# Moving the bias add and the lower ELU branch of an eight-head attention layer from VectorE to GpSimd

## The reference

```python
x = _layernorm(x + L0(x))   # relational GCN, three layers
x = _layernorm(x + L1(x))   # GCN, two layers
x = _layernorm(x + L2(x))   # graph attention, 4 heads of 256, then 1 head of 768
x = _layernorm(x + L3(x))   # graph attention, 8 heads of 96, then 1 head of 768
```

```python
h = (x @ W).reshape(n, heads, out_c)
e = leaky_relu(al_s[src] + al_d[dst], 0.2)
ex = jnp.exp(e - segment_max(e, dst)[dst])
alpha = ex / (segment_sum(ex, dst)[dst] + 1e-16)
out = segment_sum(h[src] * alpha[:, :, None], dst) + bias
h = jax.nn.elu(out)          # out where out > 0, exp(out) - 1 elsewhere
```

## Time and profile before

| | |
|---|---|
| median of three runs | 1627.55 us (1625.88 to 1627.65) |
| the profiled execution | 1625.69 us |
| its span | 1624.0 us |
| mean granted TensorE clock | 0.95 |
| busy: TensorE | 1468.5 us, 90% |
| busy: VectorE | 803.1 us, 49% |
| busy: ScalarE | 427.7 us, 26% |
| busy: GpSimd | 501.6 us, 31% |

### The profile page before, as it was taken

The page is one execution under the profiler, slowest core; times in us unless marked ns, Lnnn a source line. Parts: engine busy times, 40 slices in busy tenths (PEclk is TensorE's granted clock), DMA queues, the critical chain, the costliest instruction groups (busy, mean ns, idle before and its releaser), DMA issues.

```text
span 1624.0 us, 23395 instructions
## 1 busy us (share of the span) xinstructions
PE 1468.5 (90%) x8072; PEld 1347.3 (83%) x8072; DVE 803.1 (49%) x1940; ACT 427.7 (26%) x1009; POOL 501.6 (31%) x574
## 2 busy tenths in 40 slices
PE   5899799999999999999999998988699788778896
PEld 3567699999999999999998897976589748677773
DVE  7888644224534465732234444175522053588544
ACT  1153511101000001001012214345523442544422
POOL 5111322332424443344234221471116441200020
PEclk9998899999999999999999998999899899777998
DMA  3110111212342232422122112221012200100001
GB/s 115 38 30 14 36 39 30 59 41 77 103 131 84 83 113 78 137 68 59 30 59 68 40 32 67 81 69 33 1 52 59 64 10 24 44 1 1 10 1 47
DMA packets 57526, 86.53 MB, mean 53 GB/s; under 512 B 6437, under 2 KB 54053, under 8 KB 57303
## 3 DMA queue, kind: packets, MB, share of 16 engines
q1 hardware_dynamic: 45184, 66.02, 14.0%
q10 hardware_dynamic: 12244, 19.17, 3.9%
HBM read 83.24 MB, written 1.92 MB: 52 GB/s over the span
## 4 chain that ended last, share of the span: by engine, by line
PE 74%; DVE 15%; ACT 5%; issue 3%; DMA 1%; POOL 1%; DVEq 0%; ACTq 0%; SPq 0%
PE psum L2005 12%; PE psum L2008 11%; PE psum L2009 11%; PE psum L2022 7%; PE psum L2025 7%; PE psum L2418 7%; PE psum L2343 3%; PE psum L2347 3%; PE psum L2348 3%; PE psum L2110 2%; ACT psum L1059 2%; PE psum L2407 1%; DVE onehot_dst L1314 1%; DVE max_scratch L1759 1%; PE psum L2066 1%
## 5 line engine op out<-in xcount | busy, mean ns | idle before, releaser
L2005 PE MATMUL psum<-w_lo,xT_hi 128*125 128x384 f32 (+1 forms) x1110 | 382.0, 344 | 6.8 <-ACT packed_sums L867 3.2
L2008 PE MATMUL psum<-w_hi,xT_lo 128*125 128x384 f32 (+1 forms) x1110 | 377.8, 340 | 0.0
L2009 PE MATMUL psum<-w_hi,xT_hi 128*125 128x384 f32 (+1 forms) x1110 | 377.2, 340 | 0.0
L741 POOL CAST w_hi<-w_raw 128x384 fp32r<-128x384 f32 x190 | 102.8, 541 | 502.6 <-PE psum L2009 492.5
L754 POOL TENSOR_TENSOR w_lo<-w_raw,w_hi 128x384 fp32r<-128x384 f32 x106 | 108.2, 1050 | 432.7 <-ACT w_hi L1037 321.4
L1350 DVE TENSOR_TENSOR h_lo<-psum,h_hi 125x384 fp32r<-125x384 f32 (+1 forms) x120 | 66.9, 558 | 316.3 <-ACT h_hi L895 315.3
L2005 PEld LDWEIGHTS psum<-w_lo,xT_hi 128*125 128x125 f32 (+1 forms) x1110 | 209.2, 188 | 9.3 <-ACT packed_sums L867 3.7
L2008 PEld LDWEIGHTS psum<-w_hi,xT_lo 128*125 128x125 f32 (+1 forms) x1110 | 209.1, 188 | 0.1
L2009 PEld LDWEIGHTS psum<-w_hi,xT_hi 128*125 128x125 f32 (+1 forms) x1110 | 208.6, 188 | 0.0
L2022 PE MATMUL psum<-h_lo,adjacency 125*125 125x384 f32 (+3 forms) x600 | 204.3, 340 | 1.8 <-ACT adjacency L935 1.7
L743 POOL TENSOR_TENSOR w_lo<-w_raw,w_hi 128x384 fp32r<-128x384 f32 x190 | 200.7, 1056 | 15.2
(11 more groups left out here) (284 smaller groups left out, 2244.7 us busy)
## 6 DMA issues: line engine op xcount, KB each, us to landing
w_raw<-weights_dram SPq DMA_DIRECT2D x296, 192.0 KB, 2.4
score_w_raw<-weights_dram ACTq DMA_DIRECT2D x58, 192.0 KB, 2.9
x_nat<-x_dram SPq DMA_DIRECT2D x1, 1875.0 KB
x_residual<-x_dram SPq DMA_DIRECT2D x1, 1875.0 KB
out_dram<-x_residual SPq DMA_DIRECT2D x5, 375.0 KB
score_a_rows<-L_gnn_a_src_dram ACTq DMA_DIRECT2D x8, 192.0 KB, 3.4
score_a_rows<-L_gnn_a_dst_dram ACTq DMA_DIRECT2D x8, 192.0 KB, 4.7
rgcn_bias<-rgcn_bias_dram SPq DMA_DIRECT2D x1, 1125.0 KB
```

The costliest lines, as they stand in the source:

```text
L741: nc.gpsimd.tensor_copy(mem.wh[:, slot, :], mem.raw[:, raw_slot, :]).then_inc(w_hi_ready, 1)
L2005: ins = nc.tensor.matmul(o, h, wl, start=(j == 0), stop=False, skip_group_check=True)
L2008: nc.tensor.matmul(o, l, wh, start=False, stop=False, skip_group_check=True)
L2009: ins = nc.tensor.matmul(o, h, wh, start=False, stop=stop and j == k - 1, skip_group_check=True)
```

## The change

For each head GpSimd now adds the bias, after VectorE's multiplication (part_read), and tells ScalarE (elu_in). When the exponential is there (elu_out) GpSimd makes its lower branch, min(e, 1) - 1, and tells VectorE through a new semaphore, elu_low. VectorE only joins the branches. The splits of the weight chunks, which GpSimd did in one go ahead of this, are put between the heads: index 15 ahead of head 0, 16 to 19 ahead of head 1, 20 ahead of head 2, the last three after head 7.

```diff
@@ gpsimd
             split_to(Q2.chunk + 15)
-            split_to(Q2.end + AHEAD)
+            pool.wait_ge(params_loaded, 16 * 9)
+            for h in range(HEADS3):
+                split_to(min(Q2.chunk + 16 + 4 * h, Q2.end + AHEAD))
+                e, t = mem.elu[0:BP, h % 2, :, :], strip(h)
+                b = mem.par[1][0:BP, h * C3:(h + 1) * C3].rearrange("p (a c) -> p a c", a=1).to_broadcast([BP, NB, C3])
+                pool.wait_ge(part_read, Q2.unit0 + h + 1)
+                nc.gpsimd.tensor_tensor(t, t, b, ALU.add).then_inc(elu_in, 1)
+                pool.wait_ge(elu_out, h + 1)
+                nc.gpsimd.tensor_scalar(e, e, 1.0, -1.0, ALU.min, ALU.add).then_inc(elu_low, 1)
             split_to(NCHUNKS)
@@ vector
                 nc.vector.tensor_tensor(t, head_out(h)[:, :, 0:C3], mem.z[0:BP, :, h % 2:h % 2 + 1].to_broadcast([BP, NB, C3]),
                                         ALU.mult).then_inc(part_read, 1)
-                dve.wait_ge(part_read, Q2.unit0 + h + 1)
-                b = mem.par[1][0:BP, h * C3:(h + 1) * C3].rearrange("p (a c) -> p a c", a=1).to_broadcast([BP, NB, C3])
-                nc.vector.tensor_tensor(t, t, b, ALU.add).then_inc(elu_in, 1)
 
             def head_elu(h):
 
-                dve.wait_ge(elu_out, h + 1)
+                dve.wait_ge(elu_low, h + 1)
                 e, t = mem.elu[0:BP, h % 2, :, :], strip(h)
-                link(nc.vector.tensor_scalar(e, e, 1.0, -1.0, ALU.min, ALU.add))
                 nc.vector.scalar_tensor_tensor(t, t, 0.0, e, ALU.max, ALU.add).then_inc(layer_ready, 1)
```

More of the change, by code:

```diff
@@ L544, in program @@
         elu_out = sem("elu_out")
+        elu_low = sem("elu_low")
         T_Q = [T_L1 + (1 + i) * UNITS for i in range(4)]
```

## The result

The changed kernel takes 1643.53 us, the median of four runs (1642.37 to 1643.74), against 1627.60 us of the kernel before on the same chip: a ratio of 1.0099, with a 95% interval of 1.0086 to 1.0111. It is 16 us slower. The prediction had 1629.6 us and a range up to 1635.0 us, so the time lies 8.5 us above the range. The profiled execution took 1643.74 us with a span of 1642.0 us, 18.0 us above the span before. One execution of add_alone, a kernel of this study, took 5510.57 us and is left out of its ratio.

The account below looks back on a forecast made before the run. No engine alone was the bound, but a loop of handoffs with VectorE's part largest. Loop -1.1, splits +2.3 and tail +0.9 summed to +2.1 us, from a median of 1627.55 to 1629.6 us; range 1621.0 to 1635.0 us.

Parts of the forecast that it names:

- The low branch: GpSimd's min(e, 1) - 1 in each head: 0.68 us, scaled from a cast, with bounds of 0.41 and 1.22 us.
- J: Start of VectorE's joining instruction in each head; its moves were to sum to -1.1 us over the loop.
- E: End of ScalarE's exponential in each head; the join could not start before E + 0.78 us.
- its step: Forecast move of the join's start in heads 0 to 5: -0.28, -0.39, +0.11, +0.11, -0.27, -0.39 us.
- rival A: Slower: GpSimd's low branch costs 1.22 us, deciding from about 0.85 us on; 1633.8 us in all, chance 0.20.
- The splits: Five weight splits moved behind low branches block the joins of heads 0 and 1 and a L1829: +2.3 us, bounds 0 and 4.
- the sum: Loop -1.1, moved splits +2.3 and tail +0.9 us: +2.1 us in all, median 1629.6 us.
- rival C: TensorE's clock: three more groups of sums at the low level give 1632.9 us (chance 0.13), three fewer 1626.3 us (0.10).
- the tail: Serial stretch behind the last head up to TensorE's next-layer transposes: add +0.56, low branch +0.27, handoffs +0.07, together +0.9 us.
- B: Faster: VectorE's own work is the bound, 7.9 us go and the tail's 0.9 comes; 1620.6 us, chance 0.15.
- The add: GpSimd's bias add in each head: 1.22 us, with its blocking of VectorE put at nothing.
- The joins of heads 0 and 1: VectorE's joins, each waiting 0.9 us for a moved split, were to last about 1.5 us.

Follow-up runs that it names:

- add_alone: Changed kernel with VectorE making the low branch again, so GpSimd only adds the bias, and the splits made first: 1626.84 us, ratio 0.9998.
- splits_alone: Kernel before with only the weight splits moved between the heads, VectorE doing all its old work: 1638.29 us, ratio 1.0070.
- low_fast_first: Changed kernel with multiply and add for minimum and add in GpSimd's low branch, and the splits made first: 1627.96 us, ratio 1.0007.
- low_fast: Changed kernel with multiply and add for minimum and add in GpSimd's low branch, splits still between the heads: 1634.69 us, ratio 1.0056.
- the two fused kernels: Kernel before without a separate low branch, the join giving ELU plus 1: bias add on VectorE 1624.9 us, on GpSimd 1621.85 us.
- splits_first: Changed kernel with the splits of chunks 15 to 20 back in one run ahead of head 0: 1640.69 us, ratio 1.0082.
- low_alone: Changed kernel with VectorE adding the bias again, so GpSimd only makes the low branch, and the splits made first: 1641.9 us, ratio 1.0097.

## Why the prediction was wrong

**The low branch: the step that failed.** The prediction bounded it by 0.41 us and GpSimd's two-input 1.22 us and took 0.68 us from the cast. It takes 1.81 us. The upper bound rested on the unspoken idea that one input can't cost more than two, and the nearest row was nearest in shape, not in kind: a cast, where the low branch is a minimum and an add. GpSimd's groups of the kernel before have one pair of neighbours on the same tiny shape that speaks against the bound (L727 compares f16 values with a scalar, L728 adds two tensors):

```profile
L727 POOL TENSOR_SCALAR block_after<-iota,block_first_tile 1x84 f32<-1x84 f16 x3 | 2.9, 950 | 0.3
L728 POOL TENSOR_TENSOR tile_block<-tile_block,block_after 1x84 f32<-1x84 f32 x3 | 1.1, 351 | 0.3
```

So a scalar form can cost more than a two-input one, by 0.60 us here. But L725, the same comparison once more, took 0.56 us, and on 12 elements a multiplication with a constant (L731, 0.38 us) is cheaper than an add of two tensors (L732, 0.42 us). These rows could have widened the bound; they don't give the price. That 1.22 + 0.60 makes 1.82 us is luck, since L727 is another operation on another type.

**J, with the right price.** The formula "new J = E + 0.07 + low branch + 0.03" holds. Put 1.81 for 0.68 us (+1.13) into the prediction's own steps and read to join comes out as follows:

| head | its step + 1.13 us | measured |
|---|---|---|
| 0 | +0.85 | +0.88 |
| 1 | +0.74 | +0.76 |
| 2 | +1.24 | -0.75 |
| 3 | +1.24 | +0.72 |
| 4 | +0.86 | +0.88 |
| 5 | +0.74 | +1.88 |

Heads 0, 1 and 4 agree within 0.03 us. In head 2 all 47 sums and transposes between read and join ran at 2.4 GHz, where all 34 had the low level before, in head 3 21 of 39 had it after 34 of 34: both come out sooner, by 2.5 us together against the step. In head 5 L1838 waits 0.61 us for the transposes and then lasts 1.01 us beside GpSimd's add. Head 6's join ends at 1538.64, where its sums would have let VectorE go on some 0.9 us sooner: next read +0.94 us, the point that rival A had named with +0.4.

**The splits.** The blocking was sized well: +2.3 us forecast, 2.2 us measured (0.79, 0.78 and 0.67 us for 0.9, 0.9 and 0.5). But the term priced only the blocked instructions, not what a longer wait does to TensorE behind it. That is the second step that failed, and it holds for the low branch's delay as well: the sum put the clock at nothing and left it to rival C. The stretch join to row got 6.6 us for the clock, and splits_alone shows 2.9 us of blocking followed by 3.8 us of clock in one head.

Between the first read and the next layer the sum had +2.1 us and the traces have +16.6. Of the 14.5 us between them 6.9 lie in the steps to the join and 1.15 in the tail, both of which the low branch's price lengthens, and 6.5 in join to row, where the clock is.

**Rivals.** A had the direction and the mechanism and named its deciding point, 0.85 us, but its price stopped at 1.22 us, and its 0.54 us per head went unamplified: 1633.8 us. With 1.81 us in its own arithmetic (1.13 us in six heads, 1.13 in the tail, 0.95 in head 6) it gives 1629.6 + 8.9 = 1638.5 us; the clock's 6.6 us make 1645.1 us. With the 2.5 us that heads 2 and 3 came sooner and the 1.1 us that head 5 came later it is 1643.7 us, for 1643.5 measured. All but A's own terms are read from the trace of the changed kernel, so this closes the account and doesn't test it. B fell at once: VectorE's busy time fell by 3.5 us of 20 and the loop grew. C counted groups at the low level as if all places were equal. Their number moved by a tenth (198 matmuls for 180); their place did most, and C's price of three groups was half of what the place cost.

**What held.** The add takes 1.20 us (1.49 where it waits behind L1838) and costs nothing beside VectorE; in heads 0 to 4 L1838 is not lengthened by it. The joins of heads 0 and 1 last 1.45 and 1.44 us. The tail has the structure forecast: +2.05 us, which is its 0.9 + 1.13.

```profile
1539.72 1.20 POOL L847 TENSOR_TENSOR residual_product<-residual_product,par 125x480 f32<-125x480 f32 x1 [1.77 <-DVE residual_product L1917]
1540.95 0.60 ACT L1197 ACTIVATE elu_exp<-residual_product 125x480 f32<-125x480 f32 x1 [4.90 <-POOL residual_product L847]
1541.64 1.81 POOL L849 TENSOR_SCALAR elu_exp<-elu_exp 125x480 f32<-125x480 f32 x1 [0.72 <-ACT elu_exp L1197]
...
1543.48 0.66 DVE L1924 SCALAR_TENSOR_TENSOR residual_product<-residual_product,elu_exp 125x480 f32<-125x480 f32 x1 [3.85 <-POOL elu_exp L849]
```

With a low branch of 0.59 us and the splits first, the two mis-sized terms are gone, and what remains of the prediction's sum is -1.1 + 0.9 - 0.09 x 7 = -0.8 us; low_fast_first measured +1.1 us with an interval from -0.5 to +2.9. The remaining sum lies just outside this interval, and it is that near only in total: in low_fast_first's profile, which at 1630.69 us is 2.7 us above the median, read to join is 2.2 us shorter and join to row 5.6 us longer, 47 of its 114 matmuls there at the low level. The clock that the sum leaves out stays.

**What stays open.** Which of the short stretches gets the low level isn't explained by the idling ahead of it. In add_alone's head 1 TensorE idled only 1.76 us and ten sums took 1.94 us, some of them at the low level; in low_fast_first's head 1 it idled 2.17 us, about what it had idled in head 0 of before (2.16 us, then 1.00 throughout), and got 0.50:

```profile
1449.76:1457.72 7.96, 7.96 (x30) 6.54 (x30) 1.83 (x4) 1.11 (x4) 0.00 (x0) 0.50 0.01 2
```

So the 6.6 us are shown to be the clock's, in one profiled execution of each kernel. Join to row is longer in every variant, from 2.2 us in add_alone to 8.9 us in low_fast (blocking included), also where the join came sooner; only the two fused kernels keep it within 0.9 us. Why the low level falls on just these stretches is not shown.

## What to carry to other kernels

Price a moved instruction by rows of its own operation on the new engine, the very pair of minimum and add, not by the engine's cheapest row of that length; where no row has it, call the price open and don't bound it by another kind, or time the one instruction first. An engine with no work has no free time for an instruction that stands between two others in a chain of handoffs: the bias add, which had slack, moved for nothing, and the low branch, which had none, cost 13 to 16 us with the splits in their old place (splits_first and low_alone), for the 8 x 0.40 = 3.2 us that it took off VectorE. And a delay ahead of the engine with two clock levels is to be priced with what that engine does next at the lower one: look for how the low level's stretches lie to the critical ones, not at its mean.

## What the runs showed of the hardware

**GpSimd's scalar operations.** On 480 fp32 elements a partition, minimum and add in one instruction take 1.81 to 1.83 us, a single minimum, add or multiplication 1.41 to 1.42 us, multiplication and add together 0.59 us, a copy 0.59 us, and the add of two tensors 1.20 us. Low_fast's group shows the cheap form in eight heads:

```profile
L849 POOL TENSOR_SCALAR elu_exp<-elu_exp 125x480 f32<-125x480 f32 x8 | 4.7, 591 | 27.3 <-ACT elu_exp L1197 27.3
```

The page GPSIMD Engine Reference of the Trainium skill, section 4.1 Engine selection, calls one-input operations "roughly line-rate" and two-input ones about twice as slow as VectorE's. The first holds here for the copy and for multiplication with add (0.59 us against VectorE's 0.41 us for the low branch); a single minimum, add or multiplication took 1.41 us, and for minimum with add the measurement, 1.81 us, says more than four times VectorE's time; the measurement decides. The second agrees: 1.20 us for 0.66.

**Blocking by turns.** While GpSimd runs subtractions of 1.0 us back to back, VectorE's instructions whose operands all lie in SBUF wait for them in turn: by 0.73, 0.74, 0.79 and 0.67 us in splits_alone's head 0, and two of these have only 5 elements a partition. A fifth, again of 5 elements and directly behind the second, took 0.15 us. GpSimd's instructions are lengthened too: in the changed kernel four such subtractions took 4.75 us, for 4.02 in splits_alone. Two count products beside such splits in the changed kernel's head 0 (L1801, from 1434.39), which read PSUM, keep the 0.73 us that they have without. The page SBUF — State Buffer, section Who interferes with whom, of the Trainium skill gives the mutual exclusion as a rule; by that rule, the trace agrees for the four, and the fifth fits only if it shared the second's turn, which no run shows.

**The clock.** The same 30 matmuls behind a VectorE release took 4.21 us (granted 1.00), 5.85 us (0.71) or 7.96 us (0.50), in kernels that differ by a few microseconds of delay ahead of them. In splits_alone 2.9 us of blocking brought 3.8 us of clock in one head, and five splits moved cost 11.4 us in the whole kernel.
